# Residual rows loaded tile by tile by ScalarE, and query and key weights split by rows behind the value stagings

## The reference

```python
xn = _layernorm(x)                          # x is [2, 1024, 512]
qkv = xn @ w_attn + b_attn                  # 16 heads of 32; q and k get a rotary turn
scores = einsum('bhtd,bhsd->bhts', q, k)    # causal
attn = softmax(scores) * 512 ** -0.5
o = (attn @ v) @ w_proj + b_proj
# mixture of 8 experts, the best 2 of each token, inner width 352
act = silu(g) * u ; expert_out = act @ w2 ; ffn = sum over the 2 chosen
return x + o + ffn
```

## Time and profile before

| | |
|---|---|
| median of 3 runs | 957.33 us (950.41 to 961.78) |
| profiled execution | 952.79 us |
| its span, first to last instruction | 950.9 us |
| PE busy | 853.8 us, 90% |
| DVE, ACT, POOL busy | 38%, 30%, 29% |
| mean granted clock of TensorE | 0.944 |

### The profile page before, as it was taken

One profiled execution on the slowest core, in us unless ns is written; L12 is line 12 of the kernel. 1 busy time (PEld: TensorE's weight loads), 2 busy tenths in 40 slices (PEclk: granted clock), 3 DMA queues, 4 the chain that ended last, 5 costly groups with the idle time before them and its releaser, 6 DMA issues. The chain is left out here.

```text
span 950.9 us, 12387 instructions
## 1 busy us (share of the span) xinstructions
PE 853.8 (90%) x3661; PEld 527.3 (55%) x3662; DVE 365.2 (38%) x1125; ACT 289.5 (30%) x616; POOL 271.1 (29%) x352
## 2 busy tenths in 40 slices
PE   3779999389899999957999998999999999999990
PEld 3668988245555555534555443466666666666650
DVE  4972552575656666644666111111111111111110
ACT  3041131104545655534555600021222222222210
POOL 4951000305223242303323250023333333333330
PEclk9889999758979999987999999999999999999995
DMA  9286596876346676692631125826364554533326
GB/s 321 100 265 190 197 322 202 254 171 223 106 141 168 182 197 154 172 279 67 154 98 41 39 77 179 270 56 157 68 157 118 102 152 105 109 66 65 65 33 198
DMA packets 76491, 143.19 MB, mean 151 GB/s; under 512 B 12704, under 2 KB 26528, under 8 KB 76384
## 3 DMA queue, kind: packets, MB, share of 16 engines
q1 hardware_dynamic: 40272, 69.88, 23.7%
q10 hardware_dynamic: 26752, 54.09, 20.3%
q0 software_dynamic: 9424, 18.69, 10.6%
HBM read 81.21 MB, written 61.15 MB: 150 GB/s over the span
## 5 line engine op out<-in xcount | busy, mean ns | idle before, releaser
L1272 ACT ACTIVATE probs<-scores_t 128x512 f32<-128x512 f32 (+3 forms) x384 | 164.0, 492 | 163.8 <-PE scores_t L1394 149.8
L867 PE MATMUL gu<-w,rows_t 128*128 x624 | 197.4, 459 | 1.1 <-DVE o_t L833 1.1
L1414 PE MATMUL o_acc<-probs,v_ones 128*64 128x512 f32 (+3 forms) x768 | 150.2, 514 | 14.7 <-POOL probs L1217 14.7
L1371 PE MATMUL maxima<-k_stack,q_stack 96*128 96x512 f32 (+3 forms) x384 | 143.1, 393 | 15.0 <-DMA q_stack<-qk_hi 9.0
L867 PEld LDWEIGHTS gu<-w,rows_t 128*128 128x128 f32 x624 | 115.2, 190 | 69.7 <-issue 19.7
L1394 PE MATMUL scores_t<-q_stack,k_stack 98*128 98x512 f32 (+3 forms) x384 | 140.0, 390 | 4.8 <-DMA q_stack<-row_lo 2.6
L1297 DVE CUSTOM_DVE_ANT_0 masked_scores<-maxima,mask_m 128x128 f32<-128x128 f32 (+3 forms) x256 | 121.4, 485 | 25.1 <-PE maxima L1371 20.7
L1301 DVE TENSOR_REDUCE mx<-maxima 128x1 f32<-128x512 f32 x128 | 88.2, 689 | 104.4 <-PE maxima L1371 104.2
L1394 PEld LDWEIGHTS scores_t<-q_stack,k_stack 98*128 98x128 f32 x384 | 74.1, 195 | 67.7 <-issue 44.9
L885 PE MATMUL down<-w,hidden_t 128*128 (+1 forms) x234 | 107.0, 592 | 0.8 <-DVE hidden_t L841 0.8
L1371 PEld LDWEIGHTS maxima<-k_stack,q_stack 96*128 96x128 f32 x384 | 78.1, 205 | 35.9 <-DVE mx L1301 9.6
(11 more groups left out here) (148 smaller groups left out, 895.6 us busy)
## 6 DMA issues: line engine op xcount, KB each, us to landing
w<-in_w_t SPq DMA_DIRECT2D x8, 1408.0 KB, 6.5
routed<-blank_row ACTq DMA_DIRECT2D x20, 514.0 KB, 7.4
rows<-routed ACTq DMA_DIRECT2D x39, 256.0 KB
qk_hi<-st_hi SPq DMA_DIRECT2D x32, 256.0 KB, 5.1
qk_lo<-st_lo SPq DMA_DIRECT2D x32, 256.0 KB, 6.7
q_stack<-qk_hi ACTq DMA_DIRECT2D x32, 256.0 KB, 4.5
k_stack<-qk_hi ACTq DMA_DIRECT2D x26, 256.0 KB, 5.5
v_all<-o_t SPq DMA_DIRECT2D x4, 1536.0 KB, 5.7
```

Of the source, the lines that this page charges most:

```text
L867: last = nc.tensor.matmul(gu[r][j][:, 0:I], rows_t[r][:, k * P:(k + 1) * P], w1[:, bass.ds(e, 1), k, j * I:(j + 1) * I].rearrange("p o n - ...
L1272: nc.scalar.activation(probs[:, k % PR, h, 0:w], scores_t[e % RING][:, 0:w], ACT.Exp).then_inc(exp_done, 1)
L1371: nc.tensor.matmul(mb[at % RING][:, 0:w], q_st[i][0:3 * HD, h, t * P:(t + 1) * P], k_st[i][0:3 * HD, h, c * CH:c * CH + w], start=True, st ...
L1414: last = nc.tensor.matmul(o_acc[c][2 * HD * h:2 * HD * (h + 1), CH - w:CH], v_st[i][:, j, h:h + 2, :].rearrange("p o d -> p (o d)"), probs ...
```

## The change

It has two parts that share no instruction.

**Attention.** SP no longer waits for the scatter and no longer loads the residual rows; it keeps the load of `bp`. ACT loads them in 16 DMAs of one tile each (256 KB), one behind each of the steps k = 0 to 3 of rounds 9 to 12, the first behind a wait for the scatter. A pair of tiles has its own semaphore, and POOL waits for the pair whose bias it adds.

**Projection.** The cosine product goes to a place of its own (the still empty `w_proj`), so that it need not wait for POOL. Sum, rounding and subtraction go by the four row blocks k of 512 columns, staggered by two (`qk_split`), and each has its own count. On DVE `statistics(1)` and the second group now stand behind `values(0, 7)`, the first group behind `values(0, 1)`; `statistics(2)` and `(3)` and the last inverse move behind products 1 to 3. PE waits for each k apart.

```diff
@@ projection, GpSimd
                 for k in range(DK):
                     for j in range(2):
                         last = nc.gpsimd.tensor_tensor(t[:, k, :, j], pair[:, k, :, 1 - j], sign[:, :, j], ALU.mult)
-                last.then_inc(turn_done, 1)
+                    last.then_inc(turn_done, 1)
@@ projection, ScalarE
             def qk_high(i):
                 lo, hi = parts[1 + i]
-                act.wait_ge(sum_done, i + 1)
-                nc.scalar.copy(w_hi[:, :, lo:hi], w_raw[:, :, lo:hi]).then_inc(wqk_hi_done, 1)
+                for k in range(DK):
+                    act.wait_ge(sum_done, i * DK + k + 1)
+                    nc.scalar.copy(w_hi[:, k, lo:hi], w_raw[:, k, lo:hi]).then_inc(wqk_hi_done, 1)
...
-            take_root(TPC, 2 * TPC, 2)
             qk_high(0)
-            take_root(2 * TPC, NT, NCH)
...
                     if j == 0:
+                        take_root(TPC, 2 * TPC, 2)
+                    if j == 1:
                         qk_high(1)
+                    if j == 3:
+                        take_root(2 * TPC, NT, NCH)
@@ projection, VectorE
-            def qk_sum(i):
+            def qk_cos(i):
...
-                dve.wait_ge(turn_done, i + 1)
-                link(V.tensor_tensor(w, w, cos_row[:].unsqueeze(1).to_broadcast([P, DK, D]), ALU.mult))
-                V.tensor_tensor(w, w, turned[i], ALU.add).then_inc(sum_done, 1)
...
+                dve.wait_ge(w_in[1 + i], 16)
+                V.tensor_tensor(turned_cos[:], w_raw[:, :, lo:hi], cos_row[:].unsqueeze(1).to_broadcast([P, DK, D]),
+                                ALU.mult).then_inc(cos_done, 1)
+
+            def qk_sum(i, k):
...
+                V.tensor_tensor(w_raw[:, k, lo:hi], turned_cos[:, k, :], turned[i][:, k, :], ALU.add).then_inc(sum_done, 1)
+
+            def qk_split(i):
+                for k in range(DK + 2):
+                    if k < DK:
+                        qk_sum(i, k)
+                    if k >= 2:
+                        qk_low(i, k - 2)
...
+            qk_cos(0)
             for c in range(NCH):
                 for v in range(2 * TPC):
-                    if c == 0 and v == 0:
-                        qk_sum(0)
+                    values(c, v)
+                    if c == 0 and v == 1:
+                        qk_split(0)
+                    if c == 0 and v == 7:
                         statistics(1)
-                    values(c, v)
...
+                        qk_cos(1)
+                        invert(TPC, 2 * TPC, 2)
+                        qk_split(1)
@@ attention, SyncE
                 if n == BIAS_ROUND - 1:
-                    sp.wait_ge(scattered, 16 * TOPK * NT)
                     sp.dma_start(bp[:], b_proj.partition_broadcast(P)).then_inc(bp_in, 16)
-                    for b in range(B):
-                        sp.dma_start(res[:, b * TQ:(b + 1) * TQ, :], x[b].rearrange("(a p) d -> p a d", p=P)).then_inc(res_in, 16)
@@ attention, GpSimd
-                    pool.wait_ge(res_in, 16 * B)
+                if a % 2 == 0:
+                    pool.wait_ge(res_in[a // 2], 32)
@@ attention, ScalarE
+                    if k < FIRST_LOAD and 0 <= (n - BIAS_ROUND + 1) * FIRST_LOAD + k < NT:
+                        a = (n - BIAS_ROUND + 1) * FIRST_LOAD + k
+                        if a == 0:
+                            act.wait_ge(scattered, 16 * TOPK * NT)
+                        act.dma_start(res[:, a, :], x[a // TQ, a % TQ * P:(a % TQ + 1) * P, :]).then_inc(res_in[a // 2], 16)
```

More of the change, by code:

```diff
@@ L85, in project_qkv @@
         turned = [keep["o_t"][:, i, :].rearrange("p (k n) -> p k n", n=D) for i in range(2)]
+        turned_cos = keep["w_proj"]
         small = m.sbuf("small", [P, 8, QK_TILES], F32)
@@ L150, in project_qkv @@
         wv_hi_done, wv_done = m.sem("wv_hi_done"), m.sem("wv_done")
-        turn_done, sum_done = m.sem("turn_done"), m.sem("sum_done")
+        cos_done, turn_done, sum_done = m.sem("cos_done"), m.sem("turn_done"), m.sem("sum_done")
         wqk_hi_done, wqk_done = m.sem("wqk_hi_done"), m.sem("wqk_done")
@@ L332, in turned_low, with qk_low @@
                                 ALU.subtract).then_inc(xt_done, 1)
-            def qk_sum(i):
+            def qk_cos(i):
                 lo, hi = parts[1 + i]
-                w = w_raw[:, :, lo:hi]
-                dve.wait_ge(turn_done, i + 1)
-                link(V.tensor_tensor(w, w, cos_row[:].unsqueeze(1).to_broadcast([P, DK, D]), ALU.mult))
-                V.tensor_tensor(w, w, turned[i], ALU.add).then_inc(sum_done, 1)
-            def qk_low(i):
-                lo, hi = parts[1 + i]
-                dve.wait_ge(wqk_hi_done, i + 1)
-                V.tensor_tensor(w_lo[:, :, lo:hi], w_raw[:, :, lo:hi], as_f32(w_hi[:, :, lo:hi]), ALU.subtract).then_inc(wqk_done, 1)
+                dve.wait_ge(w_in[1 + i], 16)
+                V.tensor_tensor(turned_cos[:], w_raw[:, :, lo:hi], cos_row[:].unsqueeze(1).to_broadcast([P, DK, D]),
+                                ALU.mult).then_inc(cos_done, 1)
+            def qk_sum(i, k):
+                lo, hi = parts[1 + i]
+                if k == 0:
+                    dve.wait_ge(cos_done, i + 1)
+                dve.wait_ge(turn_done, i * DK + k + 1)
+                V.tensor_tensor(w_raw[:, k, lo:hi], turned_cos[:, k, :], turned[i][:, k, :], ALU.add).then_inc(sum_done, 1)
+            def qk_low(i, k):
+                lo, hi = parts[1 + i]
+                dve.wait_ge(wqk_hi_done, i * DK + k + 1)
+                V.tensor_tensor(w_lo[:, k, lo:hi], w_raw[:, k, lo:hi], as_f32(w_hi[:, k, lo:hi]), ALU.subtract).then_inc(wqk_done, 1)
+            def qk_split(i):
[4 more added lines that the diff above has]
+                        qk_low(i, k - 2)
             def values(c, v):
@@ L451, in _ @@
                                            as_f32(st_hi[:, j % STG, :]), ALU.add, ALU.subtract).then_inc(st_ready, 1)
-                    if c == 0 and i == 0:
-                        qk_low(1)
-                    if i == 1:
+                    if c == 0 and i == 1:
+                        statistics(2)
+                    if c == 0 and i == 2:
+                        statistics(3)
+                    if i == 2:
                         shift_logits(c)
-                    if c == 0 and i == 2:
+                    if c == 0 and i == 3:
                         invert(2 * TPC, NT, 3)
@@ L514, in queries_keys @@
                 out = bank_of("qk", c, i)[:]
-                if c == 0 and i % NG == 0:
-                    pe.wait_ge(wqk_done, i // NG + 1)
                 cols = slice(i * P, (i + 1) * P)
                 for k in range(DK):
+                    if c == 0 and i % NG == 0:
+                        pe.wait_ge(wqk_done, i // NG * DK + k + 1)
                     nc.tensor.matmul(out, w_hi[:, k, cols], xt_hi[c % 2][:, k, :], start=(k == 0), stop=False)
@@ L1031, in attend @@
         scaled = m.sem("o_scaled")
-        bp_in, res_in, biased = m.sem("bp_early_in"), m.sem("res_early_in"), m.sem("biased_early")
+        bp_in, res_in, biased = m.sem("bp_early_in"), [m.sem(f"res_in{i}") for i in range(NT // 2)], m.sem("biased_early")
         proj_full, res_done = m.sem("proj_early_full"), m.sem("res_early_done")
```

## The result

The changed kernel takes **931.86 us** (median of 4 runs, 929.16 to 932.23), the kernel before in the same comparison 956.53 us (950.41 to 961.78, 4 runs): a ratio of 0.974, 95% interval 0.968 to 0.980. It is faster by 2.6%, and the time lies 4 us under the 936 forecast. The profiled execution took 932.23 us with a span of 930.4, against 952.79 and 950.9 before; TensorE's mean granted clock is 0.957 against 0.944.

A forecast was written before the change was run, and what follows sets the result against it. PE, busy 90% of the span, was held by waits, in the projection by VectorE. 952.79 - 15.3 - 3.3 = 934.2 us from the profiled execution, 938.7 from the median; forecast 936 in between, range 926 to 947.

The forecast's parts named there:

- Attention, 15.3 us forecast: Round 9 is 16.8 us too long; removing that, less 1.5 us for stretched `share_rows`, gains 15.3 us.
- the one named: Round 9: `share_rows`, issued behind 4 MB of residual loads on SP's queue, land in 18.6 instead of 5.0 us.
- The charge of 1.5 us: Rounds 9 and 11: residual tiles on ScalarE's queue stretch `share_rows`; cost 1.5 us, bounds 0 and 4.4.
- The issues, forecast at 0: ScalarE's 16 added tile issues, 0.43 us each, 7 us in all, lie beside other work and cost 0.
- The slower side: Rival: ScalarE is caught in tile issues of 2.83 us on a backed up queue, 978 us in all; chance 0.05.
- Projection, 3.3 us forecast: VectorE works without waits through the split; chunk 1's values begin at about 66.3 instead of 69.64, gaining 3.3 us.
- the 9.9 + 4.8 of the forecast: Projection's sixteen VectorE slices: 9.9 us of work from start to start, plus 4.8 us for meeting POOL.
- a toll of 0.3 us: Projection: each of 16 VectorE slices loses 0.3 us meeting POOL in SBUF, 4.8 us; bounds 0 and 22.1.
- The second rival: Projection: VectorE and POOL take turns, slices wait out POOL operations, 22.1 instead of 4.8 us, 951.5 in all; chance 0.08.
- the row at 35.10: Earlier trace, projection: POOL began at 35.10, VectorE at 35.24 with its undisturbed 2.28 us, while POOL took 4.22.
- the one on the holes: PE in chunk 0: the 6.3 us hole is filled, as two value products come first and `claim` finds its banks.
- Table load: Projection: the exponential's table load before `st_hi` of product 4 is charged in full, 1.28 us, bounds 0 and 3.

The follow-up runs named there:

- the second profile: The changed kernel run once more, unaltered, for another profile and more runs: 933.87 us (6 runs), interval of the ratio 0.976 to 0.984.
- The late rotation: Changed kernel, but POOL rotates the second group's weights only after the first group's last subtraction: 929.45 us, ratio 0.977.
- the bulk on ScalarE: Changed kernel, but ScalarE loads the residual in two whole 2048 KB DMAs behind k = 0 of round 9: 936.98 us, ratio 0.988.
- the tiles on SP: Changed kernel, but SP issues all sixteen 256 KB residual tiles in round 9 at the old place: 947.3 us, ratio 0.996.
- the spread on SP: Changed kernel, but SP issues the residual tiles, four in each of rounds 9 to 12: 932.76 us, ratio 0.979.
- the last experiment: Changed kernel, but POOL's second rotation follows the first group's last subtraction and SP issues the tiles, four a round: 930.49 us, ratio 0.978.

## Why the prediction was right, step by step

**Attention, 15.3 us forecast.** Round 9 became 16.0 us shorter in the profile, and the part alone gave 14 us of median. The cause was the one named, and three experiments tell it from its neighbours. The charge of 1.5 us for tiles that stretch `share_rows` was not due: they land in 4.8 us in round 9 and 5.0 in round 11, as in the undisturbed round of the earlier trace rows. The prediction had the tiles overlap them; in fact a tile landed in 2.7 us (2.4 to 4.4), so the last of round 9, issued at about 396.2, was in at about the time when `share_rows` went out at 399.08. Half of the charge was eaten by a term that the prediction did not have: round 9 takes 20.3 us and not 19.49, because PE waits 0.76 us for `row_lo`. With 1.34 us of the same wait and the low clock behind it the round took 23.9 us in the second profile, so a part of the near hit is luck.

**The issues, forecast at 0.** 334 to 358 ns each, below the 0.43 taken from SP's row. The slower side needed 1.26 us.

**The rule on the queues.** `share_rows` took 18.6 us behind 4 MB on their own queue and 6.9 us with the same 4 MB on ScalarE's. The Trainium skill (DMA: Bandwidth & Descriptors, "Issuing engines are not separate DMA queues") says that DMAs of all issuers interleave on the same engines and that another issuer saves only sequencer time. The 6.9 us do not agree with the second half: here the issuer decided what waited behind what. The stretch from 5 to 6.9 us agrees with the first half.

**Projection, 3.3 us forecast.** 4.5 us in the profile at the first value product of chunk 1, 3 us in the whole time of the part alone. The sum came out, and so did its largest unknown, the slices: 9.4 + 5.2 = 14.7 us with the rounding, the 9.9 + 4.8 of the forecast. That they agree is luck: it is an average over two cases that were not told apart. I spread a toll of 0.3 us evenly; in fact the first group paid about 0.6 us a slice ((9.4 - 5.0) / 8) and the second group nearly nothing. The second rival was therefore half right: of its bound of 0.83 us a slice against rotations two thirds came true, its 1.94 a slice against normalizing was wrong, and the row at 35.10 had said so, with POOL taking the loss. The late rotation shows the cause by removing it. The Trainium skill (SBUF — State Buffer, "Who interferes with whom") says that a VectorE instruction with two SBUF inputs and a GpSimd one that reads SBUF exclude each other; slices of 0.68 us that take 1.35 beside the rotation agree with that. The normalizing does not agree: POOL's operation took 3.50 us instead of 2.07, and VectorE's slices filled all of that time at their undisturbed pace but for one, so the two were not held off each other for a whole instruction.

**The step that failed** is the one on the holes. The forecast had PE's hole before value product 6 gone and took the two value products ahead of the split to be enough for `claim`. The hole moved instead: with the first group's split at 9.4 us, PE ran out of banks and stood 4.35 us before the first query and key product, and its clock then stood at 0.50 from 33 to 38.2 us. Two more waits of 3.1 us in all, for `st_lo` before products 6 and 7, were not in the forecast either. The hole cost nothing against the sum, since the sum was made on VectorE, which had no idle time there. But it is the place where 2 us more were to be had.

**Table load.** The 1.28 us were charged in full; VectorE waited 0.71 us for that `st_hi`. The end of `xt_lo(1)` came at 64.54 instead of 66.15, and the slices have no part in that. VectorE began at 21.06 instead of 21.3, and up to 64.54 it was busy for 42.01 us where the forecast has 38.75 + 4.8 = 43.55: the two cosine products took 2.35 + 2.26 us instead of 2.93 + 2.60, and one step of the inverse deviation 0.16 instead of 0.69. The sum had carried these over from before as they were.

**What the forecast could not hold.** The third row of the table of events: in both kernels PE waits exactly 2.35 us for VectorE's `mx`, and the 15 us behind it ran at different clocks. Before (stretch, PE busy, PE loads, VectorE, ScalarE, POOL busy, granted clock):

```profile
260.00:267.00 7.00, 6.41 (x15) 3.11 (x16) 2.92 (x14) 1.36 (x3) 3.32 (x6) 0.50 0.50 174
267.00:275.00 8.00, 8.00 (x27) 4.18 (x25) 3.89 (x10) 3.89 (x7) 0.91 (x1) 0.58 0.53 165
```

After:

```profile
256.00:263.00 7.00, 6.29 (x25) 2.87 (x25) 3.88 (x17) 2.06 (x4) 3.38 (x5) 0.76 0.56 193
263.00:271.00 8.00, 8.00 (x38) 4.08 (x36) 4.75 (x18) 4.59 (x11) 1.79 (x3) 1.00 0.81 223
```

That gave 3.6 us. The other profiles show that the one of before is the exception here: from the store at 259.06 to the one at 273.66 it takes 14.6 us, and the same distance is 9.4 to 12.1 us in all eleven others, the two with the projection of before and the new attention among them (10.9 and 11.0). At the start of the experts it went the other way: behind the same wait of 2.6 us the clock was 1.00 before, and 0.50 and then 0.64 after, for 3.1 us. From the first to the fourth load of expert weights it takes 12.0 us in before and in the runs with the projection part alone, the bulk on ScalarE, the tiles on SP and the spread on SP, but 13.7 to 15.1 us in all six profiles with the tiles on ScalarE, and 13.7 in the last experiment, which has them spread on SP. Whether the change has a hand in these 1.7 us is open. One profile against another thus carries 3 us at such a place, and the first of the two belongs to neither kernel. The median of four runs, 931.86, lies 2.3 us under the 934.2 of the sum, that of the six later ones, 933.87, on it. The 936 lay higher because half of the distance to a median of 957.33 was added to the sum; in the later comparisons before had 951, below the 952.79 of its profile, so this step pointed the wrong way.

## What to carry to other kernels

A small load that somebody needs soon must not be issued behind megabytes on the same queue: move the bulk to a queue whose next loads have slack, or spread it over rounds; cutting it into pieces alone did next to nothing here. When a long wait is gone, look for a short one in its place: here 0.8 to 1.7 us for `row_lo`. When an engine's work is cut into short instructions to overlap with a neighbour, ask what POOL does in just that stretch, and price the turns per instruction by POOL's own instruction there, not by an average over the program. And when a bottleneck engine is filled without gaps, look at which of its results the next engine wants first: VectorE was fully busy, and PE still stood 4.4 us for a bank.

## What the runs showed of the hardware that was not expected

- Waits of PE as short as 1.28, 1.34 and 1.42 us were followed by stretches at a mean granted clock of 0.61, 0.57 and 0.57, between the two levels 1.2 GHz (0.50) and 2.4 GHz (1.00), and these rounds were 4 to 6 us longer than 19.5. In other profiles of the same two kernels the waits there were 0.37 to 0.81 us and the clock stayed at 1.00, but it also stayed at 1.00 behind a wait of 1.65 us in round 9 of the spread on SP. A wait of 2.35 us was followed by some 15 us at 0.50 to 0.58 in one profile, and by 0.76 and then 1.00 in another. What decides it was not tested.
- VectorE and POOL share a loss unevenly: beside POOL's rotation (two SBUF inputs) both are stretched, a slice from 0.68 to 1.35 us and nine rotations to 11.0 us; beside POOL's normalizing (one input) POOL's goes to 3.50 us, from 2.07 and VectorE's slices keep their length. One of them took 1.10 us, but in the projection part alone the same slice took 0.72 behind a wait of 0.29 us for ScalarE, so this is at least in part a wait for the rounding.
- A queue with 4 MB ahead stretched another queue's loads of 128 KB from 5.0 to 6.9 us, and its own by 14 us.
